# Attention scores of two kinds moved to opposite 64-row halves of the matmul array, with the product of probabilities and values cut into two column halves

## What is computed

```python
q = x @ Wq.T + bq + ocr_bias;  k = x @ Wk.T + bk;  v = x @ Wv.T + bv
# 16 heads of 16 features
scores = einsum('bhsd,bhtd->bhst', q, k) / sqrt(16)
scores = scores + band_mask          # 0.1 where |s - t| <= 2
attn = softmax(scores, axis=-1)
out = einsum('bhst,bhtd->bhsd', attn, v) -> (B, S, 256) @ Wo.T + bo
x = x + out
```

## Time and profile before

| | us |
|---|---|
| median of 3 runs | 4212.57 |
| lowest and highest | 4211.86, 4222.06 |
| profiled execution, its own time | 4213.35 |
| span of the profiled execution | 4211.6 |
| PE busy | 3768.9 (89%) |
| DVE busy | 2720.6 (65%) |
| ACT busy | 1790.0 (43%) |
| POOL busy | 1364.4 (32%) |

### The profile page before, as it was taken

The page is one execution under the profiler, slowest core; times in us unless marked ns, Lnnn a source line. Parts: engine busy times, 40 slices in busy tenths (PEclk is TensorE's granted clock), DMA queues, the critical chain, the costliest instruction groups (busy, mean ns, idle before and its releaser), DMA issues. The chain is left out here.

```text
span 4211.6 us, 79961 instructions
## 1 busy us (share of the span) xinstructions
PE 3768.9 (89%) x27516; PEld 2923.9 (69%) x27516; DVE 2720.6 (65%) x5626; ACT 1790.0 (43%) x3205; POOL 1364.4 (32%) x1045
## 2 busy tenths in 40 slices
PE   6997888887997999999968899998999979999999
PEld 4886677776886888888734455554555538888888
DVE  5665677775676566666655666666676655666665
ACT  3444344443554333333325555555555553333333
POOL 2555222222665222222222323323323322222222
PEclk9998999998998999999969999999999989999999
DMA  3000000000001000000034334333333410000000
GB/s 101 0 0 14 2 0 0 0 0 1 0 0 38 1 0 0 0 0 0 10 69 90 76 67 90 83 68 86 86 68 83 90 46 6 15 10 10 15 10 16
DMA packets 72273, 131.72 MB, mean 31 GB/s; under 512 B 7776, under 2 KB 40944, under 8 KB 66048
## 3 DMA queue, kind: packets, MB, share of 16 engines
q1 hardware_dynamic: 72192, 130.65, 13.2%
HBM read 71.38 MB, written 58.72 MB: 31 GB/s over the span
## 5 line engine op out<-in xcount | busy, mean ns | idle before, releaser
L1476 DVE TENSOR_REDUCE neg_max_sb<-s_ps 128x1 f32<-128x512 f32 x1024 | 689.5, 687 | 436.0 <-PE s_ps L1217 433.1
L1382 ACT ACTIVATE prob_sb<-s_ps 128x512 f32<-128x512 f32 x1024 | 599.8, 599 | 543.4 <-PE s_ps L1229 532.7
L850 POOL TENSOR_TENSOR m_act_lo_sb<-m_act_sb,m_act_hi_sb 128x512 fp32r<-128x512 f32 x320 | 414.1, 1294 | 1042.1 <-ACT m_act_hi_sb L816 1042.1
L806 ACT ACTIVATE m_silu_sb<-moe_h_ps 128x512 f32<-128x512 f32 x320 | 191.4, 598 | 966.7 <-PE moe_h_ps L761 966.7
L1229 PE MATMUL s_ps<-q_stack_sb,k_stack_sb 97*128 97x512 f32 x1024 | 483.3, 473 | 101.5 <-DMA q_stack_sb<-neg_max_t_sb 87.2
L1134 POOL TENSOR_TENSOR prob_sb<-prob_sb,band_sb 128x520 f32<-128x520 f32 (+1 forms) x256 | 285.2, 1114 | 853.0 <-ACT prob_sb L1382 852.9
L904 DVE TENSOR_TENSOR m_act_sb<-moe_h_ps,m_silu_sb 128x512 f32<-128x512 f32 x320 | 220.6, 689 | 502.1 <-ACT m_silu_sb L806 472.4
L1229 PEld LDWEIGHTS s_ps<-q_stack_sb,k_stack_sb 97*128 97x128 f32 x1024 | 203.0, 199 | 409.4 <-ACT prob_sb L1382 239.1
L1217 PE MATMUL s_ps<-k_stack_sb,q_stack_sb 96*128 96x512 f32 x1024 | 451.8, 444 | 28.7 <-DMA k_stack_sb<-qk_scratch 16.3
L529 POOL TENSOR_TENSOR f_sq_lo_sb<-f_sq_sb,f_sq_hi_sb 128x512 fp32r<-128x512 f32 x256 | 329.6, 1296 | 349.8 <-ACT f_sq_hi_sb L504 349.7
L916 DVE SCALAR_TENSOR_TENSOR x_resident_sb<-moe_y_ps,gates_sb,x_resident_sb 128x256 f32 (+1 forms) x1024 | 422.5, 474 | 0.5
(11 more groups left out here) (282 smaller groups left out, 8904.4 us busy)
## 6 DMA issues: line engine op xcount, KB each, us to landing
qk_scratch<-qk_hi_sb SPq DMA_DIRECT2D x128, 256.0 KB
q_stack_sb<-qk_scratch SPq DMA_DIRECT2D x64, 384.0 KB, 5.2
k_stack_sb<-qk_scratch SPq DMA_DIRECT2D x64, 384.0 KB, 7.0
qk_scratch<-qk_lo_sb SPq DMA_DIRECT2D x64, 256.0 KB
x_resident_sb<-x SPq DMA_DIRECT2D x4, 2048.0 KB, 17.8
out<-x_resident_sb SPq DMA_DIRECT2D x16, 512.0 KB, 2.9
moe_w_values_sb<-routed_w SPq DMA_DIRECT2D x12, 512.0 KB, 6.5
moe_w_values_sb<-shared_w SPq DMA_DIRECT2D x6, 256.0 KB, 5.4
```

Of the source, the lines that this page charges most:

```text
L850: nc.gpsimd.tensor_tensor(al[:, slot(e), :], act_f[:, e % 2, :], as_f32(ah[:, slot(e), :]), ALU.subtract).then_inc(low_ready, 1)
L1382: nc.scalar.activation(prob[:, kt % 2, i, :], s2p[i % 2][:, :], ACT.Exp).then_inc(exp_done, 1)
L1476: nc.vector.tensor_reduce(nm[:, g % 2, i, qt:qt + 1], s1p[i % 2][:, :], AXIS_X, ALU.max, negate=True).then_inc(max_done, 1)
```

## The change

- `AHEAD` becomes 8, two whole head groups. Groups 0 and 1 now have their stacks in rows 0 to 47 and groups 2 and 3 in rows 64 to 111 (`stack_rows`). The first scores of a unit are thus always in the other 64-row half than the second scores of the same unit. `q_stack` and `k_stack` lose half of their columns.
- The first scores use 48 rows and the second 64; the maximum stands in the 49th row of a half.
- `pv` is cut into column halves of 256: the first of step st-1 at unit 2 of step st, the second at unit 0 of step st+1. `prob` gets four buffers, and the exponential waits for an older `pv`.
- Slots of the next sequence move: its transposes from (1,2), (2,1) to (1,3), (2,0); its first query and key projection from (3,2) to (4,2) to (3,1) to (4,0); `k_full` and `q_full` from (4,3) to (4,1); `high_part` from (5,1), (5,2) to (4,2), (4,3). `v_copy` goes from after (0,3) to after (1,0).

```diff
...
-XT_AT = [(1, 2), (2, 1)]
-QK_AT = [[(3, 2), (4, 0), (4, 1), (4, 2)], [(8, 0), (8, 1), (8, 2), (9, 0)]]
+XT_AT = [(1, 3), (2, 0)]
+QK_AT = [[(3, 1), (3, 2), (3, 3), (4, 0)], [(8, 0), (8, 1), (8, 2), (9, 0)]]
 OT_AT = [(6, 1), (6, 2)]
...
 V_AT = [(13, 2), (14, 1), (15, 0), (15, 2)]
-AHEAD = 7
+AHEAD = 8
 STACK = 3 * HD
-MAX_ROW = 96
+HALF_ROWS = 64
...
-        qs = core.sbuf("q_stack", [P, GROUPS, GH, TOKENS], F32R, ctx)
-        ks = core.sbuf("k_stack", [P, GROUPS, GH, TOKENS], F32R, ctx)
+        qs = core.sbuf("q_stack", [P, GROUPS // KT, GH, TOKENS], F32R, ctx)
+        ks = core.sbuf("k_stack", [P, GROUPS // KT, GH, TOKENS], F32R, ctx)
         one_f = core.sbuf("one_f", [P, 1], F32, ctx)
...
         vaug = core.sbuf("v_ones", [P, TILES, HEADS, 2 * HD], F32, ctx)
-        prob = core.sbuf("prob", [P, 2, GH, TOKENS], F32, ctx)
+        prob = core.sbuf("prob", [P, TILES, GH, TOKENS], F32, ctx)
         ot = core.sbuf("o_t", [P, TOKENS], F32, ctx)
...
+        def stack_rows(g, n):
+            return slice(HALF_ROWS * (g // 2), HALF_ROWS * (g // 2) + n)
         with nc.Block() as block:
...
                     for x, stack in enumerate((qs, ks)):
-                        sp.dma_start(as_f32(stack[0:STACK, g, :, :]),
+                        sp.dma_start(as_f32(stack[stack_rows(g, STACK), g % 2, :, :]),
                                      scratch[m, x, :, :, heads, :]).then_inc(loaded[g], 16)
...
                     sp.wait_ge(nmt_ready, b * GROUPS + g + 1)
-                    sp.dma_start(as_f32(qs[MAX_ROW:MAX_ROW + 1, g, :, :]), as_f32(nmt[:, g % 2, :])).then_inc(rowed[g], 16)
+                    row = stack_rows(g, STACK).stop
+                    sp.dma_start(as_f32(qs[row:row + 1, g % 2, :, :]), as_f32(nmt[:, g % 2, :])).then_inc(rowed[g], 16)
...
                     off = lo - (kt * P - BAND)
-                    pr = prob[:, kt % 2, :, lo:hi]
+                    pr = prob[:, kt, :, lo:hi]
                     nc.gpsimd.tensor_tensor(pr, pr, bcast(band[:, off:off + hi - lo].unsqueeze(1), [P, GH, hi - lo]),
...
                     pe.wait_ge(max_done, (b * STEPS + st) * GH + i + 1)
-                    r = slice(0, MAX_ROW)
-                    nc.tensor.matmul(s1p[i % 2][:, :], qs[r, g, i, qt * P:(qt + 1) * P], ks[r, g, i, :],
+                    r = stack_rows(g, STACK)
+                    nc.tensor.matmul(s1p[i % 2][:, :], qs[r, g % 2, i, qt * P:(qt + 1) * P], ks[r, g % 2, i, :],
                                      start=True, stop=True).then_inc(s1_ready, 1)
...
                     pe.wait_ge(exp_done, (b * STEPS + st) * GH + i + 1)
-                    r = slice(0, MAX_ROW + 1)
-                    nc.tensor.matmul(s2p[i % 2][:, :], ks[r, g, i, kt * P:(kt + 1) * P], qs[r, g, i, :],
+                    r = stack_rows(g, HALF_ROWS)
+                    nc.tensor.matmul(s2p[i % 2][:, :], ks[r, g % 2, i, kt * P:(kt + 1) * P], qs[r, g % 2, i, :],
                                      start=True, stop=True).then_inc(s2_ready, 1)
...
-                def pv(b, st):
+                def pv(b, st, half):
                     g, kt = st // TILES, st % TILES
-                    pe.wait_ge(band_done, b * STEPS + st + 1)
-                    if st == 0:
-                        pe.wait_ge(v_ready, b + 1)
-                    if kt == 0 and not (first(b) and g == 0):
-                        pe.wait_ge(ot_ready, b * GROUPS + g)
+                    c = slice(half * DM, half * DM + DM)
+                    if half == 0:
+                        pe.wait_ge(band_done, b * STEPS + st + 1)
+                        if st == 0:
+                            pe.wait_ge(v_ready, b + 1)
+                        if kt == 0 and not (first(b) and g == 0):
+                            pe.wait_ge(ot_ready, b * GROUPS + g)
                     for i in range(GH):
-                        op = nc.tensor.matmul(pvp[2 * HD * i:2 * HD * (i + 1), :], vaug[:, kt, GH * g + i, :], prob[:, kt % 2, i, :],
-                                              start=(kt == 0), stop=(kt == TILES - 1))
-                    op.then_inc(pv_done, 1)
+                        op = nc.tensor.matmul(pvp[2 * HD * i:2 * HD * (i + 1), c], vaug[:, kt, GH * g + i, :],
+                                              prob[:, kt, i, c], start=(kt == 0 and half == 0), stop=(kt == TILES - 1),
+                                              skip_group_check=True)
+                    if half:
+                        op.then_inc(pv_done, 1)
...
                             at = (st, i)
-                            if i == 3 and st:
-                                pv(b, st - 1)
-                            elif i == 3 and before:
-                                pv(b - 1, STEPS - 1)
+                            if i == 2 and st:
+                                pv(b, st - 1, 0)
+                            elif i == 2 and before:
+                                pv(b - 1, STEPS - 1, 0)
+                            if i == 0 and st > 1:
+                                pv(b, st - 2, 1)
+                            elif i == 0 and before:
+                                pv(b - 1, STEPS - 2 + st, 1)
                             if st % TILES == 1 and i == 1:
...
                 last = core.batches - 1
-                pv(last, STEPS - 1)
+                pv(last, STEPS - 2, 1)
+                pv(last, STEPS - 1, 0)
+                pv(last, STEPS - 1, 1)
                 out_t(last, GROUPS - 1)
...
                     act.wait_ge(s2_ready, n * GH + i + 1)
-                    if i == 0 and not (first(b) and st < 2):
-                        act.wait_ge(pv_done, n - 1)
-                    nc.scalar.activation(prob[:, kt % 2, i, :], s2p[i % 2][:, :], ACT.Exp).then_inc(exp_done, 1)
+                    if i == 0 and not (first(b) and st < TILES):
+                        act.wait_ge(pv_done, n - TILES + 1)
+                    nc.scalar.activation(prob[:, kt, i, :], s2p[i % 2][:, :], ACT.Exp).then_inc(exp_done, 1)
...
                             exp_unit(b, st, i)
-                            if st == 0 and i == 3:
+                            if st == 1 and i == 0:
                                 v_copy(b)
...
                                     ot_copy(b - 1, GROUPS - 1)
-                            if more and (st, i) in ((4, 3), (9, 1)):
+                            if more and (st, i) in ((4, 1), (9, 1)):
                                 k_full(b + 1, st // 8)
...
                                 norm.high(act, b + 1, lambda: act.wait_ge(v_ps, b + 1), range(i - 1, i))
-                            if more and (st, i) in ((5, 1), (5, 2), (9, 2), (9, 3)):
-                                high_part(b + 1, st // 8, int((st, i) in ((5, 2), (9, 3))))
+                            if more and (st, i) in ((4, 2), (4, 3), (9, 2), (9, 3)):
+                                high_part(b + 1, st // 8, int(i == 3))
                             if before and (st, i) in ((6, 3), (7, 0)):
...
                                 norm.low(dve, b + 1, range(st - 2, st - 1))
-                            if more and (st, i) in ((4, 3), (9, 1)):
+                            if more and (st, i) in ((4, 1), (9, 1)):
                                 q_full(b + 1, st // 8)
...
```

## The result

The changed kernel takes 4376.15 us (median of 4 runs, 4358.85 to 4386.57) against 4214.43 for the kernel before: a ratio of 1.0377, 95% interval 1.034 to 1.0413, or 162 us more. The forecast was 4270 and a range to 4345. The direction was right; the forecast had 57 us more, about a third of what came. The profiled execution has a span of 4384.8 us.

A forecast was written before the change was run, and what follows sets the result against it. TensorE was taken to set the pace, with waits for transfers. Fifteen cycles of 3.5 us structure plus 0.3 pace, less 0.4 once per launch, gave +57 us on 4213.35: 4270 us, range 4170 to 4345.

The forecast's parts named there:

- Priced at nothing: List of effects given no cost, among them the granted clock's fall to half after each long wait.
- The structure: Cycle of four segments per sequence: first scores wanted at (8,0), a step earlier, +3.5 us a cycle at unchanged pace.
- A and C: Cycle segments fixed by transfers: high parts ready to first key stack, 19.0 us; second high parts' writes to (12,0), 11.7.
- B: Elastic segment from first key stack landing to second high parts' writes; takes in step 8, from 4.9 to 12.1 us.
- D: Elastic segment from (12,0) to the next cycle; loses 3.7 us through earlier high parts, from 45.2 to 41.5.
- Pairing: A unit's two scores, in different row halves, stream together, saving 0.235 us a unit: -9.9 us a cycle.
- next pair "0.235 later": Sign of pairing in the profile after: a unit's two scores start within some hundredths, the next pair 0.235 us later.
- Rival 3: The two scores do not overlap, so the 9.9 us a cycle is not earned: 4418 us, chance 0.07.
- Layout changes: Leaving an array layout and returning costs 0.34 us: +3.7 a cycle for pv halves, +4.4 for projections and transposes.
- Rival 1: Layout changes between row halves and full rows are free, the 4.4, 1.5 and 0.6 go: 4172 us, chance 0.24.
- pairs out of step: After a layout change a pair's two scores start apart by up to the exposed load, about 0.1 us: +1.5 a cycle.
- The wait at (3,1): The projection moved from (3,2) to (3,1) waits on VectorE for the low part: +0.6 us a cycle.

The follow-up runs named there:

- e1_lead_only: The kernel before with only the lead of 8 steps and the moved slots, scores on all rows, pv whole: 4298.31 us, ratio 1.0200.
- e2_pv_whole: The changed kernel with pv whole, 512 columns at unit 3, and v_copy back at (0,3): 4383.03 us, ratio 1.0396.
- e5_same_half: As e2_pv_whole, but all four groups' stacks in rows 0 to 47, so both scores share a half, and prob has two buffers: 4900.22 us, ratio 1.1630.
- e9_filler3: The changed kernel with overwritten filler matmuls in waits: 24 at (8,0), 10 at (12,0), 6 before the projection at (3,1): 4270.80 us, ratio 1.0153.
- e12_early_row3_first: The kernel before, lead 7, with all moved slots of the change and group 3's row of maxima ahead of the writes for groups 2 and 3: 4130.70 us.
- e4_filler: The changed kernel with overwritten filler matmuls in two waits: 30 before the first scores at (8,0), 10 before the second at (12,0): 4327.45 us, ratio 1.0270.

## Why the prediction was wrong

**The step that failed** is in "Priced at nothing": the granted clock falls to half after each long wait, and "there are two such waits before and after". There are three after, counting the projection of step 3, and they are followed by far more slow time, 30.2 us a sequence for 8.8. Taking the low clock away with fillers is worth 105 us in the changed kernel (4376 to 4271) and 15 in the kernel before, so the term priced at nothing is 90 of the 162 us. I had rows with the clock at 0.57 and read them as something that both kernels have. What was missing is that slow time grows with the wait before it (step 8: 4.0 us before, 9.4 in e1_lead_only), and more with the way the array is used: e1_lead_only and e2_pv_whole have waits for the keys of nearly the same length, and 13.9 and 31.3 us of low clock. Step 3 shows it best. In the changed kernel:

```profile
3017.04 0.62 PE L1194 MATMUL tp_ps<-xnT_hi_sb,Wq_hi_sb 128*128 128x512 f32 x1 [1.26 <-DVE xnT_lo_sb L158]
3017.45 0.63 PE L1194 MATMUL tp_ps<-xnT_hi_sb,Wq_lo_sb 128*128 128x512 f32 x1
```

A wait of 1.26 us, and the next matmuls 0.41 apart: the clock falls at a wait that is half of what the kernel before took at (8,0). e1_lead_only waits up to 1.1 us at the same place, with scores on all rows, and has no low clock in step 3; e2_pv_whole, with row halves and `pv` whole, waits up to 1.3 us and has 4.3 us of it.

**The structure** was right in its place and too cheap in its size. A and C stayed at 19.2 and 11.5 us, step 8 came out of the transfers' cover, the wait at (8,0) is for the key stack, 7.34 us, and B was 12.2 in e1_lead_only for 12.1. But the high parts came 1.45 us earlier there, not 3.7, and D lost 1.3 us where 3.1 were forecast: the work moved on ScalarE and the moved transposes had not been counted.

**Pairing** happens: the two loads and the two matmuls start within 0.01 us. The next pair "0.235 later" that the prediction named as a sign was not seen: no pair follows another by less than 0.33, as each has a change of layout before it or waits for its exponential. That a pair takes no longer than one score matmul shows at its end: `pv` starts 0.33 after a pair (3006.33 to 3006.66) as it did after a single one before (3002.80 to 3003.13). What pairing is worth by itself, 9.9 us a cycle in the forecast, no run separated, as e5_same_half lost its clock. Its net with the prices of the layout can be read: D is 41.9 us in e9_filler3 and 41.4 in e12_early_row3_first, which has the same slots, scores on all rows and next to no low clock in D. So halves and pairs together gain nothing, as the forecast had it (-0.3). Rival 3 is out.

**Layout changes** are not free in rows either: 0.38 us for one and back, the forecast's 0.34 slightly small. Rival 1 is out. The rule of the Trainium skill in "TensorEngine Tiling (Array Packing)", Key Properties, that changing the tiling mode drains TensorE, agrees with the 0.38 in so far as a change costs time. The term for pairs out of step (+1.5) was wrong: after a change their two weight loads overlap, and only the 0.10 already in the price is seen. Pairs do start out of step elsewhere, where one of the two waits for its buffer.

**The wait at (3,1)** was +0.6 and is about that: steps 3 and 4 of e1_lead_only are 0.66 us longer together.

**The sum.** The term for `pv` is 0.34 x 10.5 = 3.6 and stands as 3.7, which makes 2 us in the launch. Without the clock the forecast was 3.8 us a cycle more than before. e9_filler3 has 84.2 - 80.3 = 3.9, and its 4271 us are the forecast's 4270, but that is luck: it compares 4.8 us of low clock with 8.8. With fillers in both kernels the difference is 84.2 - 78.9 = 5.3, 1.5 more than forecast. The term that was off is D's loss of 3.7, which was too large.

**Open:** what in the row halves brings the low clock. The matmuls have fewer rows, but TensorE also waits more often for exponentials between the pairs. e5_same_half has the low clock without such waits, which speaks for the rows, but it changed other things as well; e4_filler and e9_filler3, whose fillers use all 128 rows, change both at once.

## What to carry to other kernels

When a matmul engine waits for a transfer of fixed length, moving its consumer earlier in the schedule lengthens the wait by all the work that used to lie inside; count the cycle in segments, fixed and elastic, before counting instructions. Price the clock as a term of its own, by the slow time behind each wait, and do not assume that it stays as it was when a change lengthens a wait or puts the matmuls on fewer rows. Fillers in the wait are a cheap test of it; put them into both kernels before you compare. When a slot is moved, count what every engine has to do there, not TensorE alone. A small transfer that gates the next phase belongs ahead of the large ones in its queue: here that alone was worth 41 us.

## What the runs showed of the hardware

- Two matmuls on opposite 64-row halves, 48 and 64 rows deep and 512 columns wide, start within 0.01 us of each other, loads included. A pair of them takes as long as one: `pv` starts 0.33 us after either. The closest next pair came 0.33 us later.
- Going between halves and full rows, or halves and column strips, costs 0.38 us for both ways at the full clock, about 0.10 of it the exposed load. Between full rows and column strips it was 0.34.
- In e5_same_half TensorE, busy for all of 11 us with scores on 48 and 64 rows one after the other and `pv` between, had a granted clock of 0.50, and 0.56 over 125 us; in the kernel before, with scores on 96 and 97 rows, it had 0.96 over 80 us.
- After a wait of 7.34 us the clock was still low 8 us after work had begun again, in the changed kernel. In the kernel before, after waits of 2.4 to 2.9 us, it was low for 4.0 to 4.4 us in the mean.
- After a wait of 1.1 us the clock stayed high with scores on all rows (e1_lead_only); after 1.3 us it fell with scores on row halves (e2_pv_whole), for 4.3 us.
